# Opening batches of a fused LRU, attention and MoE kernel: u turned two batches ahead, v a batch later in y's banks, half of the normalised rows by ScalarE

## The chip, the cores and the metric

One Trainium2 chip, one core. The metric is the device time of the launch in microseconds; lower is better. The kernel before takes 1007.23 us (median of three runs, 1007.21 to 1008.69).

## The reference

x has 4 batches of 1024 tokens with 128 channels, all in float32. Two residual blocks follow each other:

```python
x = x + lru(layernorm(x))          # Bu = u B^T, scan with Lambda over the 1024 tokens, y = Re(C x) + D u
x = x + ffn(layernorm(x))
# ffn(a):
h = a + attention(rmsnorm(a, ln1_w))        # 16 heads of 8 channels, softmax over 1024 tokens
h = h + moe(rmsnorm(h, ln2_w))              # 8 experts, 256 hidden, top 2
```

The change lies in the first block and in what prepares attention: layernorm of x (called u), Bu, the scan, y, the residual sum, the second layernorm and rmsnorm in one (called a), and the projections q, k and v of a.

## The kernel before

**Stages.** The program has an opening (0 to about 160 us of the profile), in which the four batches go through the LRU and the projections, then sixteen groups of four heads ("quads") of attention, then the experts. Only the opening is touched. A batch is 8 tiles of 128 tokens. Every engine has its instruction order written out by hand, and the engines meet through semaphores that count up; a wait is for a count.

**A batch in the opening.** For batch b:

- u_nat, the normalised x, is made by VectorE for batch 0 and by ScalarE (`norm_u`, L870) for batches 1 to 3.
- TensorE turns its eight tiles into PSUM banks 0 and 1 (`first_half`, L1491), ScalarE copies them to `u_T` (`save_u`, L855), and four matmuls make Bu in banks 2 to 5 (L1498).
- VectorE (`states`, L1146) multiplies Bu by cosine and sine (L1149, L1150, from PSUM), adds the two (L1152, both operands in SBUF), scans (L1153) and multiplies the states by cosine and sine in two halves (L1156, L1157). Each half releases half of the y product (`z_ready`).
- TensorE makes y in banks 6 and 7 (`product_y`, L1511). `u_T` of the same batch is one of its operands.
- VectorE (`norm_a`, L1159) adds y to xacc (L1164), takes means and variances, forms the roots with thirteen tiny chained instructions, and writes a_nat, eight tiles (L1185). It has L1164 to L1185 and then, at once, L1149 of the next batch in its queue.
- GpSimd (`keep_z`, L574) waits for the eight tiles of a_nat and then makes zres from xacc in two instructions over the whole batch (L567, L569). After that come the lower bfloat16 parts of q and k (`lower_parts`, L584, L586), which wait for VectorE's `split_part` (L1194).
- TensorE turns a_nat into banks 0 and 1 (`turn_a`, L1536), ScalarE copies that to a_T with a scale (L899), TensorE makes q and k in banks 2 to 5 (L1541), and ScalarE rounds them to bfloat16 (L904). SyncE sends the parts to DRAM. v (`project_v`, L1547) goes to banks 0 and 1, from which ScalarE copies it into vall (L911).

**The order of TensorE.** `second_half(b)` holds, for b from 0 to 2: turn u of b + 1, Bu of b + 1, turn a of b, q and k of b, y of b + 1, v of b, and last the wait for ScalarE's copy of v:

```python
def second_half(b):
    first_half(b + 1)
    turn_a(b)
    ...
    product_y(b + 1)
    project_v(0, TILES).then_inc(v_done, 1)
    pe.wait_ge(v_saved, b + 1)
```

Since v, the turned u and the turned a share banks 0 and 1, the next batch's u can't be turned before v has been copied out. `last_half(3)` mixes the last batch's turn and projections with the first score rows of attention (L1522), the maxima of which VectorE takes (L1203), and with matmuls whose result nobody reads (L1567).

Of the kernel before, what the change touches and what calls it, by code (L numbers as in the profile page):

```python
# [10 lines left out]
ALU = mybir.AluOpType  # L11
# [58 lines left out]
def build_program(nc, x, nu2, theta2, gamma_row, b_pack, b_swap, c_re_t, c_im_t, d_t, ln1, ln2,  # L70
# [3 lines left out]
    with ctx:  # L74
# [49 lines left out]

        u_nat, u_T, a_nat, a_T = (ws[:, i, :] for i in range(4))

# [71 lines left out]
        def rows_for(t):  # L198
# [15 lines left out]
            sem(n) for n in ("u_turned", "bu_done", "y_done", "a_turned", "qk_done", "v_done"))  # L214
        uT_saved, aT_saved = sem("uT_saved"), sem("aT_saved")
        u_ready, z_ready, z_kept, a_ready = sem("u_ready"), sem("z_ready"), sem("z_kept"), sem("a_ready")
        hi_ready = sem("hi_ready")
# [607 lines left out]
        def _(act):  # L825
# [27 lines left out]
            def save_u(b):  # L853
                act.wait_ge(u_turned, b + 1)
                act.activation(u_T, bank(0, 2), ACT.Copy).then_inc(uT_saved, 1)  # L855

# [37 lines left out]

            def act_batch(b, has_next, first=False):
                if has_next:
                    save_u(b + 1)
                act.wait_ge(a_turned, b + 1)
                act.activation(a_T, bank(0, 2), ACT.Copy, scale=ln1c[:, 0:1]).then_inc(aT_saved, 1)  # L899
                if not first:  # L900
                    act.wait_ge(parts_out, b * (16 * 2 * PARTS * NQ))
                for w in range(2):
                    act.wait_ge(qk_done, b * 2 + (w + 1))
                    act.activation(parts[:, w, 0, :], bank(2 + 2 * w if has_next else 2, 2), ACT.Copy,  # L904
                                   scale=(scale, 1.0)[w]).then_inc(hi_ready, 1)
                if b + 2 < B:
                    norm_u(b + 2)
                act.wait_ge(v_done, b + 1)
                for half in range(2):
                    for j in range(NQ):  # L910
                        ins = act.activation(  # L911
                            vall[:, bass.ds(b * NQ + j, 1), half * 4:half * 4 + 4, :].rearrange("p a t c -> p (a t) c"),
                            ps[:, half, :].rearrange("p (t c) -> p t c", t=4)[:, :, 32 * j:32 * j + 32], ACT.Copy)
                ins.then_inc(v_saved, 1)

            save_u(0)
            norm_u(1)
            later_squares()
            act_batch(0, True, first=True)
            for b in range(1, B - 1):  # L920
                act_batch(b, True)
            act_batch(B - 1, False)


# [132 lines left out]
        def _(dve):  # L1057
# [101 lines left out]
            def norm_a(step, b):  # L1159
# [318 lines left out]
        def _(pe):  # L1478
# [7 lines left out]

            def first_half(b, first=False):
# [4 lines left out]
                ins.then_inc(u_turned, 1)  # L1492
                pe.wait_ge(uT_saved, b + 1)
                if not first:
                    pe.wait_ge(rest_left, b * 2)
                for i in range(2):
                    for half in range(2):
                        ins = pe.matmul(bank(2 + 2 * i + half), wB[:, i, :], u_T[:, half * 512:(half + 1) * 512],  # L1498
                                        start=True, stop=True)
                ins.then_inc(bu_done, 1)  # L1500

            def product_y(b):

                for t in range(TILES):
# [3 lines left out]
                    o = bank(6, 2)[:, c]  # L1508
                    for k, (lhs, rhs) in enumerate(((x_cos, wC[:, 0, :]), (x_sin, wC[:, 1, :]), (u_T, wD[:, :]))):
# [32 lines left out]

            def project_v(t0, t1):

                for t in range(t0, t1):
                    c = slice(t * P, (t + 1) * P)
                    ins = pe.matmul(bank(0, 2)[:, c], a_T[:, c], wv[:, :], start=(t % 4 == 0), stop=True,  # L1547
                                    skip_group_check=True)
                return ins

            def second_half(b):

                first_half(b + 1)
                turn_a(b)
                pe.wait_ge(aT_saved, b + 1)
                pe.wait_ge(bu_read, b + 2)
                for i, w in enumerate((wq, wk)):
                    project_half(w, 2 + 2 * i, 0)
                    project_half(w, 2 + 2 * i, 1).then_inc(qk_done, 1)
                product_y(b + 1)  # L1560
                project_v(0, TILES).then_inc(v_done, 1)
                pe.wait_ge(v_saved, b + 1)

# [41 lines left out]

            first_half(0, first=True)
            product_y(0)
            for b in range(B - 1):
                second_half(b)
            last_half(B - 1)  # L1610
# [279 lines left out]
```

## Time and profile before

| | |
|---|---|
| median of 3 runs | 1007.23 us |
| the profiled execution | 1007.67 us |
| its span, first to last instruction | 1005.9 us |
| around the span | 1.8 us |
| TensorE busy | 867.5 us, 86% |
| VectorE busy | 854.6 us, 85% |
| ScalarE busy | 690.2 us, 69% |
| GpSimd busy | 400.4 us, 40% |
| granted TensorE clock, mean | 0.968 of 2.4 GHz |

PE is TensorE's matmul side, PEld its weight loads, DVE VectorE, ACT ScalarE, POOL GpSimd, SP SyncE. L1152 is line 1152 of the kernel. A float32 matmul is counted as two instructions (x8 for four matmuls). The first number of a timeline row is the start in us from the span's start, the second its length, and brackets give the idle time before it with what ended it.

### The profile page before, as it was taken

The numbers are of one execution on the slowest core, as the hardware profiler recorded it, in microseconds if no ns is written. First come the engines' busy times: TensorE is split into PE (matmuls) and PEld (weight loads), VectorE is DVE, ScalarE is ACT, GpSimd is POOL, SyncE is SP. The second block draws the span as 40 slices with busy tenths as digits, with TensorE's granted clock in tenths as the row PEclk, the third lists the DMA queues.
The fourth block names the chain that finished last, engine by engine and source line by source line (L and its number), as shares of the span: only waits on it lengthen the run. The fifth ranks groups of instructions, "written<-read, shape, count | busy, mean of one in ns | idle before, by whom it ended". The sixth has DMA issues, their size and how long they took to land.

```text
span 1005.9 us, 18290 instructions
## 1 busy us (share of the span) xinstructions
PE 867.5 (86%) x5968; PEld 361.7 (36%) x5968; DVE 854.6 (85%) x1463; ACT 690.2 (69%) x1471; POOL 400.4 (40%) x621
## 2 busy tenths in 40 slices
PE   0377788999999999999999999999999999989990
PEld 0155541222222223222222322222322246588990
DVE  4978889999999998988999898898799976768663
ACT  2614313888888888888888888888788875555660
POOL 7224441011010153533615443363577503346774
PEclk9789996999999999999999999999999999999995
DMA  9997643011010110100101010110101021122346
GB/s 313 387 362 192 165 111 90 9 26 28 13 25 10 32 25 9 46 9 26 38 25 25 9 46 10 33 46 10 24 31 39 18 48 48 44 63 69 105 145 198
DMA packets 60829, 74.34 MB, mean 74 GB/s; under 512 B 9152, under 2 KB 39104, under 8 KB 60352
## 3 DMA queue, kind: packets, MB, share of 16 engines
q1 hardware_dynamic: 53936, 62.93, 21.4%
q0 software_dynamic: 4608, 9.58, 2.8%
q8 instruction: 49, 0.80, 0.3%
q10 hardware_dynamic: 2192, 0.66, 0.3%
q14 instruction: 44, 0.36, 0.1%
HBM read 28.09 MB, written 44.79 MB: 72 GB/s over the span
## 4 chain that ended last, share of the span: by engine, by line
PE 60%; DVE 25%; ACT 7%; issue 5%; ACTq 1%; POOL 1%; DMA 1%; POOLq 0%; DVEq 0%; SPq 0%
PE ps L1634 21%; DVE nmax L1203 13%; PE ps L1624 10%; PE ps L1522 9%; PE ps L1736 7%; ACT prob L961 6%; PE ps L1752 3%; PE ps L1511 3%; PE ps L1697 2%; POOL by_token L810 1%; DVE wk L1153 1%; ACTq L836 1%; PE ps L1657 1%; PE ps L1716 1%; PE ps L1498 1%
## 5 line engine op out<-in xcount | busy, mean ns | idle before, releaser
L1203 DVE TENSOR_REDUCE nmax<-ps 128x1 f32<-128x1024 f32 x512 | 601.8, 1219 | 43.9 <-PE ps L1522 39.5
L961 ACT ACTIVATE prob<-ps 128x512 f32<-128x512 f32 x1024 | 529.6, 604 | 90.6 <-PE ps L1624 89.0
L1522 PE MATMUL ps<-packs 50*128 50x512 bf16 x1024 | 343.0, 389 | 9.7 <-DVE nmax L1203 5.4
L1624 PE MATMUL ps<-packs 50*128 50x512 bf16 x1024 | 312.1, 384 | 30.2 <-ACT prob L961 20.8
L1634 PE MATMUL ps<-prob,vpad 128*32 128x512 f32 x2048 | 273.6, 606 | 0.0
L1522 PEld LDWEIGHTS ps<-packs 50*128 50x128 bf16 x1024 | 74.8, 94 | 240.4 <-DVE nmax L1203 184.9
L1624 PEld LDWEIGHTS ps<-packs 50*128 50x128 bf16 x1024 | 75.9, 94 | 144.8 <-ACT prob L961 94.1
L544 POOL MEMSET packs<- 2x2048 bf16 x32 | 57.5, 1796 | 171.1 <-PE ps L1624 169.9
L810 POOL DMA_INDIRECT by_token<-wk,vall x80 | 80.1, 1001 | 96.1 <-DVE wk L1293 61.4
L1736 PE MATMUL ps<-ws 128*128 128x128 f32 x640 | 87.2, 280 | 2.9 <-DVE ws L1313 2.1
L1736 PEld LDWEIGHTS ps<-ws 128*128 128x128 f32 x640 | 78.6, 193 | 8.7 <-issue 7.0
L1634 PEld LDWEIGHTS ps<-prob,vpad 128*32 128x32 f32 x2048 | 40.3, 108 | 60.2 <-issue 58.1
L1752 PE MATMUL ps<-w,ws 128*128 x320 | 50.6, 282 | 3.3 <-DVE wk L1293 3.1
L646 POOL TENSOR_TENSOR zres<-zres,front 128x512 f32<-128x512 f32 x6 | 7.6, 1269 | 108.4 <-ACT front L936 108.2
L1752 PEld LDWEIGHTS ps<-w,ws 128*128 128x128 f32 x320 | 42.4, 193 | 11.3 <-issue 11.2
L1004 ACT ACTIVATE ws<-ps 128x256 f32<-128x256 f32 x58 | 22.2, 383 | 32.8 <-PE ps L1736 31.8
L1286 DVE TENSOR_TENSOR ws<-ps,ws 128x256 f32<-128x256 f32 x58 | 24.5, 422 | 21.7 <-ACT ws L1004 19.2
L1511 PE MATMUL ps<-wC,wk 128*128 128x128 f32 x128 | 22.2, 301 | 21.9 <-DVE wk L1157 21.9
L1313 DVE COPY ws<-w 128x512 f32 x80 | 34.2, 430 | 7.3 <-issue 4.6
L731 POOL DMA_INDIRECT by_expert_rows<-front,slots x32 | 31.2, 976 | 11.0 <-issue 7.6
L680 POOL TENSOR_TENSOR front<-logit 128x64 f32<-128x64 f32 x24 | 6.2, 292 | 66.5 <-ACT logit L940 66.5
L1491 PE MATMUL ps<-ident,ws 128*128 128x128 f32 x32 | 5.2, 314 | 28.6 <-DVE wB L1110 25.5
(300 smaller groups left out, 857.8 us busy)
## 6 DMA issues: line engine op xcount, KB each, us to landing
by_expert_rows<-prob SPq DMA_DIRECT2D x4, 5016.0 KB, 36.8
packs<-k_parts SPq DMA_DIRECT2D x32, 192.0 KB, 3.6
packs<-q_parts SPq DMA_DIRECT2D x64, 96.0 KB, 3.1
vall<-by_expert_rows SPq DMA_DIRECT2D x80, 66.0 KB
packs<-by_token SPq DMA_DIRECT2D x8, 512.0 KB, 5.4
w<-w_t SPq DMA_DIRECT2D x3, 1024.0 KB, 10.7
q_parts<-front SPq DMA_DIRECT2D x16, 192.0 KB, 3.1
k_parts<-front SPq DMA_DIRECT2D x16, 192.0 KB, 3.4
```

The lines of the kernel that those rows point to most:

```text
L544: gp.memset(qpack[r:r + MAX_PARTS, slot, :, :, :], 0.0).then_inc(q_clear, 1)
L731: gp.indirect_dma_start(by_expert_rows, bass.IndirectOffsetOnAxis(ap=slots[:, t % 2, n % 2, n // 2:n // 2 + 1], axis=0), rows_for(t)[:, n ...
L810: gp.indirect_dma_start(by_token, bass.IndirectOffsetOnAxis(ap=dest[:, group, k:k + 1], axis=0), y_nat[:, group % YR, k * H:(k + 1) * H], ...
L961: act.activation(prob[:, v % RING, :], bank(col_bank(pos)), ACT.Exp).then_inc(col_free, 1)
L1203: dve.tensor_reduce(nmax[:, half, par, pair, qt:qt + 1], bank(first, 2), AX_X, ALU.max, negate=True).then_inc(row_free, 1)
L1313: dve.tensor_copy(w_tile[:, j % 3, :].rearrange("p (n c) -> p n c", n=2), w13[:, :, bass.ds(here[j], 1), :].rearrange("p n a c -> p n (a c ...
L1511: ins = pe.matmul(o, lhs[:, c], rhs, start=(k == 0 and t % 4 == 0), stop=(k == 2), skip_group_check=True)
L1522: ins = pe.matmul(bank(first + kh), qpack[r:r + ROWS, slot, half, pair, qt * P:(qt + 1) * P], kpack[r:r + ROWS, slot, pair, kh * HALF:(kh ...
L1624: pe.matmul(bank(col_bank(pos)), kpack[r:r + ROWS, slot, head // 2, kt * P:(kt + 1) * P], qpack[r:r + ROWS, slot, half, head // 2, :], sta ...
L1634: pe.matmul(ps[32 * head:32 * head + VW, PV_BANK, :], vpad[:, q % 2, kt, head, :], prob[:, v % RING, :], start=(kt == 0), stop=(kt == TILE ...
L1736: ins = pe.matmul(ps[:, up_bank(j), n * P:(n + 1) * P], w_tile[:, j % 3, n * P:(n + 1) * P], x_T[:, group % 2, k * P:(k + 1) * P], start=( ...
L1752: ins = pe.matmul(ps[:, y_bank(j), 0:H], hid[:, j % 4, c * P:(c + 1) * P], w2[:, bass.ds(e, 1), c, :].rearrange("p a h -> p (a h)"), start ...
```

## The change

- `u_T` becomes two buffers, taken by b % 2. TensorE turns u of batch b + 2 where it turned u of b + 1 (`turn_u`), and Bu of b + 1 (`product_bu`) finds its u_T saved long before. u of batch 1 is turned before the y of batch 0.
- v of batch b - 1 is projected in batch b, after Bu of b + 1, into y's banks 6 and 7, once VectorE has added y to xacc; the next y waits for ScalarE's copy of it. v of batch 2 stays in banks 0 and 1 after y of 3, and batch 3 is as before.
- Of the eight tiles of a_nat, VectorE makes four (tiles 0 to 3) and ScalarE the other four, each as one ACTIVATE Identity with a scale and a bias from two per-partition columns. The bias, minus mean times root, is one new VectorE instruction (`off_a`, 128x4), which also releases ScalarE (`roots_ready`).
- ScalarE's `norm_u` runs a batch earlier.

```diff
-        u_nat, u_T, a_nat, a_T = (ws[:, i, :] for i in range(4))
+        u_nat, u_even, a_nat, a_T = (ws[:, i, :] for i in range(4))
+        u_T = (u_even, sb("u_odd", [P, L])[:, :])
+        off_a = sb("off_a", [P, 2, 4])
...
-                act.activation(u_T, bank(0, 2), ACT.Copy).then_inc(uT_saved, 1)
+                act.activation(u_T[b % 2], bank(0, 2), ACT.Copy).then_inc(uT_saved, 1)
...
+            def norm_a(b):
+                act.wait_ge(roots_ready, b + 1)
+                for t in range(4, TILES):
+                    act.activation(a_nat[:, t * H:(t + 1) * H], xacc[:, b * TILES + t, :], ACT.Identity,
+                                   bias=off_a[:, b % 2, t - 4:t - 3],
+                                   scale=roots[:, b % 2, 3 * TILES + t:3 * TILES + t + 1]).then_inc(a_ready, 1)
...
+            def act_batch(b):
+                last = b == B - 1
+                if b + 2 < B:
+                    save_u(b + 2)
+                norm_a(b)
+                act.wait_ge(a_turned, b + 1)
+                act.activation(a_T, bank(0, 2), ACT.Copy, scale=ln1c[:, 0:1]).then_inc(aT_saved, 1)
+                if 1 <= b < B - 1:
+                    save_v(b - 1, 6)
+                if b:
+                    act.wait_ge(parts_out, b * (16 * 2 * PARTS * NQ))
+                for w in range(2):
+                    act.wait_ge(qk_done, b * 2 + (w + 1))
+                    act.activation(parts[:, w, 0, :], bank(2 if last else 2 + 2 * w, 2), ACT.Copy,
+                                   scale=(scale, 1.0)[w]).then_inc(hi_ready, 1)
+                if b + 3 < B:
+                    norm_u(b + 3)
+                if b >= B - 2:
+                    save_v(b, 0)
...
-                for t in range(TILES):
+                dve.scalar_tensor_tensor(off_a[:, b % 2, :], stats[:, 4:TILES, 0], -1.0, y[:, TILES + 4:2 * TILES],
+                                         ALU.mult, ALU.mult).then_inc(roots_ready, 1)
+                for t in range(4):
                     dve.tensor_scalar(a_nat[:, t * H:(t + 1) * H], tile(xacc, b, t), stats[:, t, 0:1],
                                       y[:, TILES + t:TILES + t + 1], ALU.subtract, ALU.mult).then_inc(a_ready, 1)
...
-            def second_half(b):
-
-                first_half(b + 1)
+            def batch(b):
+
+                if b + 2 < B:
+                    turn_u(b + 2)
+                product_bu(b + 1)
+                if b:
+                    pe.wait_ge(y_taken, b + 1)
+                    project_v(0, TILES, first=6).then_inc(v_done, 1)
+                if b + 2 < B:
+                    pe.wait_ge(uT_saved, b + 3)
                 turn_a(b)
                 pe.wait_ge(aT_saved, b + 1)
                 pe.wait_ge(bu_read, b + 2)
                 for i, w in enumerate((wq, wk)):
                     project_half(w, 2 + 2 * i, 0)
                     project_half(w, 2 + 2 * i, 1).then_inc(qk_done, 1)
+                pe.wait_ge(v_saved, b)
+                pe.wait_ge(y_taken, b + 1)
                 product_y(b + 1)
-                project_v(0, TILES).then_inc(v_done, 1)
-                pe.wait_ge(v_saved, b + 1)
+                if b == B - 2:
+                    project_v(0, TILES).then_inc(v_done, 1)
+                    pe.wait_ge(v_saved, b + 1)
```

TensorE between y of batch 1 and y of batch 2 (u_nat, u_T, a_nat and a_T are slices of ws), before:

```order
L1547 MATMUL ps<-wv,ws 128x128 x8
L1491 MATMUL ps<-ident,ws 128x128 [waits u_ready,v_saved]
L1491 MATMUL ps<-ident,ws 128x128 x7
L1498 MATMUL ps<-ws,wB 128x512 [waits rest_left,uT_saved]
L1498 MATMUL ps<-ws,wB 128x512 x3
L1536 MATMUL ps<-ident,ws 128x128 [waits a_ready]
L1536 MATMUL ps<-ident,ws 128x128 x7
```

and now (L1513 turns u, L1522 is Bu, L1571 v, L1560 turns a):

```order
L1513 MATMUL ps<-ident,ws 128x128 [waits u_ready]
L1513 MATMUL ps<-ident,ws 128x128 x7
L1522 MATMUL ps<-ws,wB 128x512 [waits rest_left,uT_saved]
L1522 MATMUL ps<-ws,wB 128x512 x3
L1571 MATMUL ps<-wv,ws 128x128 [waits y_taken]
L1571 MATMUL ps<-wv,ws 128x128 x7
L1560 MATMUL ps<-ident,ws 128x128 [waits a_ready,uT_saved]
L1560 MATMUL ps<-ident,ws 128x128 x7
```

v has moved from ahead of Bu to behind it, and the wait for v's copy no longer stands ahead of the turn of u.

VectorE from the last root to Bu of the next batch, before:

```order
L60 SCALAR_TENSOR_TENSOR roots<-roots 128x16 [waits dve_self]
L1185 TENSOR_SCALAR ws<-xacc,mv,roots 128x128 [waits dve_self]
L1185 TENSOR_SCALAR ws<-xacc,mv,roots 128x128 x7
L1149 TENSOR_TENSOR wk<-ps,att 128x1024 [waits bu_done]
L1150 TENSOR_TENSOR wk<-ps,att 128x1024
L1152 TENSOR_TENSOR wk<-wk 128x1024 [waits dve_self]
```

and now:

```order
L60 SCALAR_TENSOR_TENSOR roots<-roots 128x16 [waits dve_self]
L1204 SCALAR_TENSOR_TENSOR off_a<-mv,roots 128x4 [waits dve_self]
L1207 TENSOR_SCALAR ws<-xacc,mv,roots 128x128 x4
L1169 TENSOR_TENSOR wk<-ps,att 128x1024 [waits bu_done]
L1170 TENSOR_TENSOR wk<-ps,att 128x1024
L1172 TENSOR_TENSOR wk<-wk 128x1024 [waits dve_self]
```

Four of eight instructions went to ScalarE and one small one came; what used to be L1149, L1150 and L1152 is L1169, L1170 and L1172 in the changed program.

ScalarE in batch 1, before:

```order
L855 ACTIVATE ws<-ps 128x1024 [waits u_turned]
L899 ACTIVATE ws<-ps,ln1c 128x1024 [waits a_turned]
L904 ACTIVATE front<-ps 128x1024 [waits qk_done,parts_out]
L904 ACTIVATE front<-ps 128x1024 [waits qk_done]
L862 ACTIVATE ws<-xacc,rx 128x128 x8
L867 ACTIVATE ws<-ws,rx 128x128 [waits centred]
L867 ACTIVATE ws<-ws,rx 128x128 x7
L911 ACTIVATE vall<-ps 128x128 [waits v_done]
L911 ACTIVATE vall<-ps 128x128 x7
```

and now:

```order
L858 ACTIVATE u_odd<-ps 128x1024 [waits u_turned]
L902 ACTIVATE ws<-xacc,off_a,roots 128x128 [waits roots_ready]
L902 ACTIVATE ws<-xacc,off_a,roots 128x128 x3
L922 ACTIVATE ws<-ps,ln1c 128x1024 [waits a_turned]
L911 ACTIVATE vall<-ps 128x128 [waits v_done]
L911 ACTIVATE vall<-ps 128x128 x7
L929 ACTIVATE front<-ps 128x1024 [waits qk_done,parts_out]
L929 ACTIVATE front<-ps 128x1024 [waits qk_done]
```

The copy of v stands between a_T and q now, and four tiles of a_nat ahead of a_T.

## Rows read from the trace of the kernel before

**Rows 1.** Chain of waits, first two y products and batch 1's turn (start, us, what)

```profile
51.90 8.57 PE ps L1511 x48
...
76.76 5.62 PE ps L1511 x48
82.38 1.80 PE ps L1547 x16
84.20 1.47 ACT vall L911 x8
85.72 1.11 PE ps L1491 x8
...
87.93 3.71 PE ps L1498 x8
```

**Rows 2.** Timeline of VectorE, batch 0 and then batch 1

```profile
65.66 0.17 DVE L60 SCALAR_TENSOR_TENSOR roots<-roots 128x16 f32<-128x16 f32 x1
65.87 2.14 DVE L1185 TENSOR_SCALAR ws<-xacc,mv,roots 128x128 f32<-128x128 f32 x8
...
70.42 2.63 DVE L1152 TENSOR_TENSOR wk<-wk 128x1024 f32<-128x1024 f32 x1
73.08 2.29 DVE L1153 TENSOR_TENSOR_SCAN wk<-lam,wk 128x1024 f32<-128x1024 f32 x1
...
88.10 2.14 DVE L1185 TENSOR_SCALAR ws<-xacc,mv,roots 128x128 f32<-128x128 f32 x8
91.67 1.23 DVE L1149 TENSOR_TENSOR wk<-ps,att 128x1024 f32<-128x1024 f32 x1 [1.43 <-PE ps L1498]
...
94.17 1.22 DVE L1152 TENSOR_TENSOR wk<-wk 128x1024 f32<-128x1024 f32 x1
95.43 2.29 DVE L1153 TENSOR_TENSOR_SCAN wk<-lam,wk 128x1024 f32<-128x1024 f32 x1
```

**Rows 3.** Timeline of GpSimd, zres of batch 0 and batch 1

```profile
68.09 1.90 POOL L567 TENSOR_TENSOR zres<-xacc,mv 128x1024 f32<-128x1024 f32 x1 [14.33 <-DVE ws L1185]
70.07 1.90 POOL L569 TENSOR_TENSOR zres<-zres,roots 128x1024 f32<-128x1024 f32 x1
...
92.30 1.90 POOL L569 TENSOR_TENSOR zres<-zres,roots 128x1024 f32<-128x1024 f32 x1
```

**Rows 4.** Groups of ScalarE by shape, 25 to 161 us (busy us, mean ns)

```profile
L862 ACT ACTIVATE ws<-xacc,rx 128x128 f32<-128x128 f32 x24 | 7.3, 389 | 0.0
...
L885 ACT ACTIVATE vall<-xacc 128x128 f32<-128x128 f32 x16 | 4.7, 292 | 0.0
```

**Rows 5.** Timelines of VectorE and GpSimd, both in SBUF near 48 us

```profile
48.23 2.29 DVE L1153 TENSOR_TENSOR_SCAN wk<-lam,wk 128x1024 f32<-128x1024 f32 x1
...
47.69 0.57 POOL L604 TENSOR_TENSOR rx<-rx 128x16 f32<-128x16 f32 x1
48.35 2.19 POOL L605 TENSOR_TENSOR rx<-rx 128x16 f32<-128x16 f32 x1
```

**Rows 6.** Timelines of VectorE and TensorE, the end of the opening

```profile
132.80 2.14 DVE L1185 TENSOR_SCALAR ws<-xacc,mv,roots 128x128 f32<-128x128 f32 x8
134.86 4.61 DVE L1203 TENSOR_REDUCE nmax<-ps 128x1 f32<-128x1024 f32 x4
...
135.00 1.09 PE L1536 MATMUL ps<-ident,ws 128*128 128x128 f32 x8 [1.24 <-DVE ws L1185]
...
137.26 0.60 PE L1522 MATMUL ps<-packs 50*128 50x512 bf16 x2 [0.53 <-DVE nmax L1203]
...
138.24 1.02 PE L1541 MATMUL ps<-ws,wq 128*128 128x512 f32 x2
```

**Rows 7.** Timeline of ScalarE, the first exponentials of attention

```profile
167.84 4.26 ACT L961 ACTIVATE prob<-ps 128x512 f32<-128x512 f32 x8 [7.93 <-PE ps L1624]
```

**Rows 8.** Busy time of the engines in a stretch; timeline of TensorE in it

```profile
70.00:76.70 6.70, 3.67 (x8) 1.44 (x8) 6.49 (x6) 3.85 (x9) 1.90 (x1) 1.00 0.86 267
...
76.76 0.71 PE L1511 MATMUL ps<-wC,wk 128*128 128x128 f32 x4 [2.61 <-DVE wk L1157]
```

More of the change, by code:

```diff
@@ L215, in build_program @@
         uT_saved, aT_saved = sem("uT_saved"), sem("aT_saved")
+        roots_ready = sem("roots_ready")
         u_ready, z_ready, z_kept, a_ready = sem("u_ready"), sem("z_ready"), sem("z_kept"), sem("a_ready")
@@ L893, in later_squares, with save_v @@
                 act.wait_ge(squares, 1)
[L895 to L907, printed above, removed]
+            def norm_a(b):
[4 more added lines that the diff above has]
+                                   scale=roots[:, b % 2, 3 * TILES + t:3 * TILES + t + 1]).then_inc(a_ready, 1)
+            def save_v(b, first):
                 act.wait_ge(v_done, b + 1)
@@ L912, in act_batch @@
                             vall[:, bass.ds(b * NQ + j, 1), half * 4:half * 4 + 4, :].rearrange("p a t c -> p (a t) c"),
-                            ps[:, half, :].rearrange("p (t c) -> p t c", t=4)[:, :, 32 * j:32 * j + 32], ACT.Copy)
+                            ps[:, first + half, :].rearrange("p (t c) -> p t c", t=4)[:, :, 32 * j:32 * j + 32], ACT.Copy)
                 ins.then_inc(v_saved, 1)
+            def act_batch(b):
[17 more added lines that the diff above has]
+                    save_v(b, 0)
             save_u(0)
@@ L918, in _ @@
             later_squares()
[L919 to L922, printed above, removed]
+            save_u(1)
+            norm_u(2)
+            for b in range(B):
+                act_batch(b)
             def col_copy(name, q, k):
@@ L1484, in _, with turn_u @@
             pe.wait_ge(b_scaled, 4)
-            def first_half(b, first=False):
+            def turn_u(b):
                 pe.wait_ge(u_ready, b * TILES + TILES)
@@ L1492, in first_half, with product_bu @@
                 ins.then_inc(u_turned, 1)
+            def product_bu(b):
                 pe.wait_ge(uT_saved, b + 1)
-                if not first:
-                    pe.wait_ge(rest_left, b * 2)
+                pe.wait_ge(rest_left, b * 2)
                 for i in range(2):
                     for half in range(2):
-                        ins = pe.matmul(bank(2 + 2 * i + half), wB[:, i, :], u_T[:, half * 512:(half + 1) * 512],
+                        ins = pe.matmul(bank(2 + 2 * i + half), wB[:, i, :], u_T[b % 2][:, half * 512:(half + 1) * 512],
                                         start=True, stop=True)
@@ L1508, in product_y @@
                     o = bank(6, 2)[:, c]
-                    for k, (lhs, rhs) in enumerate(((x_cos, wC[:, 0, :]), (x_sin, wC[:, 1, :]), (u_T, wD[:, :]))):
+                    for k, (lhs, rhs) in enumerate(((x_cos, wC[:, 0, :]), (x_sin, wC[:, 1, :]), (u_T[b % 2], wD[:, :]))):
                         ins = pe.matmul(o, lhs[:, c], rhs, start=(k == 0 and t % 4 == 0), stop=(k == 2),
@@ L1541, in project_half, with project_v @@
                 return pe.matmul(bank(o + half), w[:, :], a_T[:, half * 512:(half + 1) * 512], start=True, stop=True)
-            def project_v(t0, t1):
+            def project_v(t0, t1, first=0):
                 for t in range(t0, t1):
                     c = slice(t * P, (t + 1) * P)
-                    ins = pe.matmul(bank(0, 2)[:, c], a_T[:, c], wv[:, :], start=(t % 4 == 0), stop=True,
+                    ins = pe.matmul(bank(first, 2)[:, c], a_T[:, c], wv[:, :], start=(t % 4 == 0), stop=True,
                                     skip_group_check=True)
                 return ins
-            def second_half(b):
-                first_half(b + 1)
+            def batch(b):
[7 more added lines that the diff above has]
+                    pe.wait_ge(uT_saved, b + 3)
                 turn_a(b)
@@ L1604, in last_half @@
                 score_unit(11)
-            first_half(0, first=True)
+            turn_u(0)
+            product_bu(0)
+            turn_u(1)
             product_y(0)
             for b in range(B - 1):
-                second_half(b)
+                batch(b)
             last_half(B - 1)
```

## The prediction

> **What bounds the kernel now.** I read the chain of waits first, because it names who is late at each handover, and of it only the opening, since nothing else is edited. In batch 1 it runs from y through v, the copy of v, the turn of u, the copy of u and Bu [rows 1], and only then reaches VectorE's L1149: 9.29 us from the end of y (82.38) to 91.67. Next, the timeline of VectorE [rows 2]. The engine is nearly always busy here. It waits 1.43 us for Bu in batch 1; in batch 0 it doesn't wait for it at all, and batch 2 repeats batch 1 to within 0.02 us in every step. So the chain through v that looks 9.29 us long is late by only 1.43 us: beside it VectorE works through the roots and L1185. Last, the timeline of GpSimd beside it, since L1152 of batch 0 takes 2.63 us where it takes 1.22 us in batch 1 [rows 2]. In batch 0 it starts at 70.42, while GpSimd's L569 runs from 70.07 to 71.97, and ends 1.08 us after that. In batch 1 GpSimd ends at 94.20 [rows 3] and L1152 starts at 94.17. The wait for Bu there has kept the two apart by chance.
>
> I count from T, the start of the instruction that follows the last root (L1185 before, off_a after). What matters is how long after T the scan starts: 7.21 us in batch 0 (73.08 less 65.87), 7.33 us in batch 1 (95.43 less 88.10) [rows 2] and in batch 2. From the scan to the next T the path isn't edited: scan, states, y, sums, roots.
>
> **Part 1: u two batches ahead, v later.** Bu of the next batch now needs only the turn of u (1.11 us, and none of it in batch 2) and Bu itself (3.71 us) after y [rows 1]: it is done 4.8 us after y's end. T comes 5.72 us after it (88.10 less 82.38) and L1149 later still. The wait of 1.43 us goes in batches 1 and 2 and nothing takes its place at Bu. v (1.80 us) follows Bu, so TensorE is free 6.6 us after y's end, that is T + 0.9, before a_nat is there (below). The copy of v (1.47 us) is queued behind a_T on ScalarE and ahead of the copy of q. It ends near T + 5.8, TensorE's q is done near T + 6.1, and y doesn't start before T + 10, so both waits for v cost nothing; if ScalarE were 4 us late y would pay. The copy of u sits ahead of the tiles of a_nat on ScalarE, and is done long before T, since a copy of that size takes about 1 us. SyncE's DMAs aren't moved.
>
> **Part 2: half of a_nat by ScalarE.** VectorE loses four of eight instructions, each 0.27 us (2.14 over 8 [rows 2]), and gains one of 128x4. A tiny one such as L60 of the roots takes 0.17 us [rows 2], of which some 0.1 stays before the next unchained one can start. L1149 thus starts at T + 0.1 + 1.07 = T + 1.17 and L1152, 2.50 us behind it (94.17 less 91.67 [rows 2]), wants to start at T + 3.67.
>
> ScalarE's price isn't in this trace: no ACTIVATE here has both a pointer scale and a pointer bias. With neither, 128x128 takes 0.292 us, with one 0.389 [rows 4]. Bounds: a second pointer costs nothing, and four take 1.26 us (a start every 0.292, as eight of L862 in 2.43 us); or it costs another 0.097 in each, unhidden, and four take about 3 x 0.39 + 0.48 = 1.64 us. I take 1.64, since the first pointer costs that much. a_nat is whole at T + 0.17 + 0.07 (a handover) + 1.64 = T + 1.88, against T + 2.14 before.
>
> The Trainium skill has a price for this (ScalarE: Activation LUTs, What ACT_TABLE_LOAD costs): about 93 ns for each pointer operand, and neighbours overlap by 93 ns. By it the four take the same 1.64 us; no row here has two pointers.
>
> **Part 3: what the gain runs into.** Without anything else the scan would start at T + 3.67 + 1.26 = T + 4.93 and the three batches would gain 2.28 + 2 x 2.40 = 7.1 us. But GpSimd's zres starts when a_nat is whole, at T + 1.96, and takes 1.90 + 0.08 + 1.90 us [rows 3]. L567 lasts to T + 3.86, and L1152 comes at T + 3.67. That is the meeting of batch 0, now in every batch. From the rows: an instruction with two operands in SBUF waits for GpSimd's to end (2.63 us, batch 0), and the reverse holds too: GpSimd's L605, 128x16, takes 2.19 us beside the scan and ends at 50.54, as the scan does at 50.52; L604 ends at 48.26, just after L1152 and as the scan starts [rows 5]. So whoever waited gets the turn at the next boundary. Then L1152 runs from T + 3.86 to T + 4.94, L569 waits for that and runs its 1.8 us to T + 6.76, and the scan, issued at T + 4.97, ends as if it had started at T + 6.61 (L1152 too ends 0.15 us sooner after a release than its full length). Against 7.21 once and 7.33 twice that is 0.60 + 2 x 0.72 = **2.0 us** of gain where 7.1 stood.
>
> What speaks for reading it so is also a rule of the Trainium skill (SBUF — State Buffer, Who interferes with whom): a VectorE instruction with two SBUF inputs and a GpSimd instruction that reads SBUF take one shared port as an exclusive lock, and the second to issue fully blocks. The trace agrees, with 2.63 us against 1.22. By this rule the sum is the one below; with no such lock it would be 7.1 + 0.8.
>
> **Part 4: the last batch.** a_nat of batch 3 is followed by VectorE's maxima. They start at T + 1.17 instead of T + 2.06 (134.86 less 132.80). The turn of a starts at T + 1.95 instead of T + 2.20, its copy ends near T + 4.2, and the fourth score row (137.26, T + 4.46), which waits for the second maximum, moves to T + 3.55. The q projection, before at T + 5.44 [rows 6], then waits for a_T and four unread matmuls (0.44 us): T + 4.66. That is **0.8 us**. Bounds: 0.9 where VectorE alone decides, 0.25 where the turn does. Behind it the opening is one chain of projections, maxima and SyncE's queue which moves as a whole, and the first exponential waits for TensorE [rows 7], not for the zero fill.
>
> **Sum.** 2.0 + 0.8 = 2.8 us. The profiled execution of 1007.67 us would be 1004.9; it stands 0.44 us above the median, so the median goes from 1007.23 to 1004.4. With ScalarE at its lower bound GpSimd starts 0.38 us sooner, and the gain becomes up to 3.6. About 0.2%, 2 us, is what a measurement of this kernel tells from no change.
>
> **The rivals.**
> - *The lock falls out badly.* L1152 waits for both L567 and L569, as happens if L569 is let in first: it ends at T + 5.84 + 1.08, the scan starts at T + 6.95, and the three batches give 0.26 + 2 x 0.38 = 1.0. For it: batch 0 of before shows just such a full wait. Against: L569 is issued 0.08 us after L567, when L1152 already waits. 1007.2 - 1.8 = 1005.4.
> - *VectorE keeps the port.* The scan is issued 0.03 us after L1152 and goes ahead of L569, which waits for both. The scan starts at T + 4.97, the gain is 2.24 + 2 x 2.36 + 0.8 = 7.8, the time 999.5. For it: all four scans take 2.29 us, none was ever held up. Against: L604, which slipped in between.
> - *The later part takes it back.* If attention started by something that isn't moved, the time would stay at 1007.2. Against: the wait of rows 7 is for TensorE.
> - *Slower: TensorE's clock.* With q and k done at T + 7.9 and y not before T + 10.2, TensorE idles 2.3 us ahead of every y, where batch 1 had 1.2. The first y, after a long idle stretch, took 8.57 us at the lower clock of 1.2 GHz, the next 5.62 us [rows 1]. If the clock fell in each of three batches it would cost 3 x 2.95 = 8.9, less 2.8: 1013.3. It decides from one batch on (2.95 against 2.8). Against: in batch 0 TensorE idled 2.61 us ahead of y with the granted clock at 1.00, that is 2.4 GHz [rows 8].
>
> **How the numbers follow.** Forecast 0.50, bad lock 0.20, port kept 0.14, taken back 0.09, clock 0.07. Time 1004.4. Faster by over 0.2% (below 1005.2) are four fifths of the forecast, the kept port and a fifth of the bad lock: 0.40 + 0.14 + 0.04, rounded up to 0.60. Slower is the clock and a little for things not seen: 0.08. The rest is 0.32. The range leaves out the kept port at its full size and the clock: 1001.0 to 1007.0, room at the lower end for a port kept in one or two batches.
>
> **What would show it.** L1149's counterpart without a wait for Bu in every batch; four ACTIVATEs of about 0.48 us; the add (L1152) longer than 1.22 us and the scan longer than 2.29 us or GpSimd's second zres instruction longer than 1.90 us in batches 0 to 2; the step from T to T, 22.23 us from batch 0 to 1 now, 0.6 to 0.7 us shorter. I am wrong if that step is 20 us (port kept), if y takes over 6 us at a clock below 1.00, or if the projections of v hold y back.

## The result and the profile after

The changed kernel takes 1005.19 us (median of ten runs, 1003.35 to 1007.06), the kernel before beside it on the same chip 1008.84 us (ten runs, 1007.19 to 1010.37). The ratio is 0.996, with a 95% interval of 0.9952 to 0.9968: 4.0 us faster, 3.2 to 4.8. That is faster by over 0.2%, as forecast. The 2.8 us of the sum lies a little below the interval. Two of the runs reported below, 1048.42 us of the kernel before on the third chip and 1330.82 us of the last variant, were in a slow state at a mean granted clock of 0.836 and 0.562, and the ratios leave them out.

| | before | after |
|---|---|---|
| profiled execution, us | 1007.67 | 1006.17 |
| span, us | 1005.9 | 1004.4 |
| T of batches 0 to 3, us | 65.87, 88.10, 110.47, 132.80 | 64.75, 87.21, 108.76, 130.31 |
| steps from T to T, us | 22.23, 22.37, 22.33 | 22.46, 21.55, 21.55 |
| first exponential, us | 167.84 | 164.54 |
| mean granted clock | 0.968 | 0.963 |

The engines' busy time, the first part of the page, hardly moves: TensorE has 4.7 us more (867.5 before), with a mean clock a little lower, and GpSimd 2.6 us more (400.4 before), which is three times the 0.86 us that its second zres instruction takes longer (below).

```profile
PE 872.2 (87%) x5968; PEld 364.4 (36%) x5968; DVE 854.3 (85%) x1451; ACT 696.9 (69%) x1487; POOL 403.0 (40%) x621
```

T is the start of the instruction after the last root, as in the prediction. The timeline of VectorE in batch 1 of the changed kernel answers to [rows 2]:

```profile
87.21 0.16 DVE L1204 SCALAR_TENSOR_TENSOR off_a<-mv,roots 128x4 f32<-128x4 f32 x1
87.29 1.11 DVE L1207 TENSOR_SCALAR ws<-xacc,mv,roots 128x128 f32<-128x128 f32 x4
88.32 1.22 DVE L1169 TENSOR_TENSOR wk<-ps,att 128x1024 f32<-128x1024 f32 x1
89.45 1.21 DVE L1170 TENSOR_TENSOR wk<-ps,att 128x1024 f32<-128x1024 f32 x1
90.81 1.31 DVE L1172 TENSOR_TENSOR wk<-wk 128x1024 f32<-128x1024 f32 x1
92.15 3.87 DVE L1173 TENSOR_TENSOR_SCAN wk<-lam,wk 128x1024 f32<-128x1024 f32 x1
96.05 0.69 DVE L1176 TENSOR_TENSOR wk<-wk,att 128x512 f32<-128x512 f32 x1
```

L1169 follows with no wait for Bu. The scan is issued at T + 4.94, and takes 3.87 us where all four took 2.29. GpSimd beside it answers to [rows 3]:

```profile
89.14 1.90 POOL L570 TENSOR_TENSOR zres<-xacc,mv 128x1024 f32<-128x1024 f32 x1 [5.40 <-ACT ws L902]
91.12 2.76 POOL L572 TENSOR_TENSOR zres<-zres,roots 128x1024 f32<-128x1024 f32 x1
```

Read the four as a queue for one door, the access to SBUF that the prediction calls the port. L570 ends at 91.04 and L1172, issued at 90.81, ends 1.08 us later. L572 is issued at 91.12 and ends at 93.88, 1.76 after L1172's end (92.12). The scan is issued at 92.15 and ends at 96.02, 2.14 after L572's end. Each waits out the other's instruction, whole. L1169 and L1170, which read PSUM, keep their 1.22 us beside L570, and L570 its 1.90.

The price of ScalarE's four tiles, in its groups by line, where [rows 4] had no such form:

```profile
L902 ACT ACTIVATE ws<-xacc,off_a,roots 128x128 f32<-128x128 f32 x16 | 6.6, 482 | 21.7 <-DVE off_a L1204 21.7
```

Batch 0 isn't shorter in this trace. The timeline of TensorE there:

```profile
66.74 1.94 PE L1560 MATMUL ps<-ident,ws 128*128 128x128 f32 x8 [3.10 <-ACT ws L902]
69.88 3.78 PE L1565 MATMUL ps<-ws,wq 128*128 128x512 f32 x4 [1.20 <-ACT ws L922]
73.46 3.12 PE L1565 MATMUL ps<-ws,wk 128*128 128x512 f32 x4
76.41 0.61 PE L1535 MATMUL ps<-wC,wk 128*128 128x128 f32 x4
```

and the busy time of the engines in two stretches of it (after the length: PE, PEld, DVE, ACT and POOL busy with counts, the granted clock, DMA share, GB/s):

```profile
66.70:76.00 9.30, 8.06 (x16) 4.11 (x17) 9.09 (x8) 2.14 (x2) 4.63 (x2) 0.50 0.79 282
76.00:82.00 6.00, 5.93 (x50) 5.50 (x48) 4.04 (x9) 5.35 (x16) 4.55 (x4) 1.00 0.98 238
```

After 3.10 us without work the granted clock is 0.50, that is 1.2 GHz, for the turn, q and most of k. q and k together take 6.70 us (69.88 to 76.58) instead of the 3.67 of [rows 8], and y begins at 76.41 (T + 11.66) though the states of its first half are ready at 74.9; in batch 1 it begins at T + 10.28. Of these 1.4 us VectorE hides 0.5, since it has the rounding of q and k to do meanwhile. The first T, on the other hand, is 1.12 us earlier than before. Two unplanned things, then, beside the planned ones; the experiments have to say which belong to the change.

The end of the opening, which answers to [rows 6] and [rows 7] (timelines of VectorE, TensorE and ScalarE):

```profile
130.31 0.16 DVE L1204 SCALAR_TENSOR_TENSOR off_a<-mv,roots 128x4 f32<-128x4 f32 x1
...
134.95 1.02 PE L1565 MATMUL ps<-ws,wq 128*128 128x512 f32 x2
...
164.54 4.26 ACT L981 ACTIVATE prob<-ps 128x512 f32<-128x512 f32 x8 [7.93 <-PE ps L1660]
```

The q projection runs at T + 4.64, and what follows moves as a whole. Attention carries the 3.3 us of its start through: the last copy of its output starts at 879.9 before and at 876.7 after. Behind it 1.7 us of the 3.2 are lost again in these two executions: from that copy to the end are 126.0 us before and 127.7 after, so that the spans differ by 1.5 us only. The 4.0 us of the runs isn't the difference of these two traces.

### The profile page after: what moved, and what is told of

It reads as the page before. It is cut to its first block, busy times and chain, and to the rows that moved or that the text cites. A ratio compares the mean times of both kernels' runs of the same rounds, so it can differ in the third digit from the quotient of the medians.

```text
span 1004.4 us, 18298 instructions
## 1 busy us (share of the span) xinstructions
PE 872.2 (87%) x5968; PEld 364.4 (36%) x5968; DVE 854.3 (85%) x1451; ACT 696.9 (69%) x1487; POOL 403.0 (40%) x621
## 4 chain that ended last, share of the span: by engine, by line
PE 58%; DVE 26%; ACT 8%; issue 5%; ACTq 1%; POOL 1%; DMA 1%; POOLq 0%; DVEq 0%; SPq 0%
PE ps L1670 21%; DVE nmax L1225 13%; PE ps L1660 9%; PE ps L1546 8%; ACT prob L981 7%; PE ps L1772 7%; PE ps L1788 3%; PE ps L1535 2%; PE ps L1733 2%; PE ps L1565 1%; DVE wk L1173 1%; POOL by_token L813 1%; ACTq L839 1%; PE ps L1693 1%; PE ps L1752 1%
## 5 line engine op out<-in xcount | busy, mean ns | idle before, releaser
L1024 ACT ACTIVATE ws<-ps 128x256 f32<-128x256 f32 x58 | 22.3, 384 | 34.3 <-PE ps L1772 33.0
L1513 PE MATMUL ps<-ident,ws 128*128 128x128 f32 x32 | 5.1, 312 | 26.3 <-DVE wB L1130 25.7
```

## The experiments

Line numbers are those of each kernel. "Before" is always measured beside the variant on the same chip. The first four are of one chip, on which the kernel before took 1009.08 us (median of 29 runs); the two other chips are marked. The second (from the two fillers to the changed kernel again) took 1065.83 us for the kernel before (median of 27). Its openings agree with the others' to about 0.2 us; of the 53 us by which the changed kernel is longer in its trace there, about 20 come between the first exponential and the last copy of attention's output and 33 behind it, where nothing is edited. Compare ratios there, and times of the opening. Each variant has one trace, so a statement on its steps is one on that execution.

**The new order alone.** The changed kernel, with all eight tiles on VectorE:

```diff
-                norm_a(b)
...
-                dve.scalar_tensor_tensor(off_a[:, b % 2, :], ...).then_inc(roots_ready, 1)
-                for t in range(4):
+                for t in range(TILES):
```

> The changed kernel with all eight tiles of a_nat made by VectorE again; u two batches ahead and v a batch later stay. Port theory (an instruction with two SBUF operands and GpSimd's zres exclude each other): L1149's counterpart no longer waits for Bu, but the add behind it then meets zres in batches 1 and 2 as it does in batch 0 of before, takes about 2.6 us, and the scan starts at T + 7.2 instead of T + 7.3: the step from T to T stays within 0.2 us of 22.37 us, and the whole kernel is within 1 us of before. Rival (the gain of the change is the wait for Bu that went): the step falls by 1.4 us in two batches, and the kernel is 2.8 us faster than before. The turn of u of batch 1 ahead of the first y should still let that y end about 1 us sooner than in before; TensorE idles over 3 us ahead of the turn of a in batch 0, so q and k there should run at the lower clock.

Measured 1008.39 us, ratio 0.999 (0.9982 to 0.9999). The timeline of VectorE, batch 1:

```profile
87.25 2.14 DVE L1204 TENSOR_SCALAR ws<-xacc,mv,roots 128x128 f32<-128x128 f32 x8
89.31 1.22 DVE L1168 TENSOR_TENSOR wk<-ps,att 128x1024 f32<-128x1024 f32 x1
...
91.80 2.62 DVE L1171 TENSOR_TENSOR wk<-wk 128x1024 f32<-128x1024 f32 x1
94.46 2.29 DVE L1172 TENSOR_TENSOR_SCAN wk<-lam,wk 128x1024 f32<-128x1024 f32 x1
```

The wait of 1.43 us is gone and the add takes 2.62 in place of 1.22, 1.40 of it given straight to the shared access. The steps are 22.25, 22.22 and 22.24 us, all of them batch 0's old step. v's move and the second u_T bring 0.1 us in batches 1 and 2 by themselves (22.22 and 22.24 for 22.37 and 22.33), and from the first T to the first exponential 0.23 us (101.74 for 101.97).

**The split alone.** The kernel before, with off_a, ScalarE's four tiles and `range(4)`:

```diff
                 save_u(b + 1)
+                norm_a(b)
...
-                for t in range(TILES):
+                dve.scalar_tensor_tensor(off_a[:, b % 2, :], ...).then_inc(roots_ready, 1)
+                for t in range(4):
```

> The kernel before with only the split of a_nat (four tiles by ScalarE, off_a). Port theory and part sum: batch 0 gains 0.6 us, batches 1 and 2 nothing, because VectorE then waits some 2.4 us for Bu (which still follows v, its copy and the turn of u), and by then zres is over; the last batch gains 0.8 us. In all 1.4 us faster than before. Rival (what counts is VectorE's busy time, four instructions of 0.27 us a batch less): 1 us in each of four batches, 4 us faster, all of what the change gives.

Measured 1009.45 us, ratio 0.9997 (0.9988 to 1.0006): nothing, where 1.4 us were expected. Batch 0 is as expected (21.55, scan 3.87), although its q is slow too (3.53 us). The next two steps are 24.04 and 24.06 instead of 22.3. Timelines of TensorE and VectorE, and the stretch of Bu:

```profile
85.99 5.40 PE L1511 MATMUL ps<-ws,wB 128*128 128x512 f32 x8 [1.11 <-ACT ws L857]
...
91.43 1.23 DVE L1160 TENSOR_TENSOR wk<-ps,att 128x1024 f32<-128x1024 f32 x1 [4.07 <-PE ps L1511]
...
86.00:89.00 3.00, 3.00 (x4) 1.36 (x5) 1.32 (x6) 1.65 (x4) 0.91 (x1) 0.53 0.36 88
```

Bu runs at the low clock for much of its length and takes 5.40 us instead of 3.71 [rows 1]. All of that lies on the path. The last batch gives its 0.8 us here too (from the last T to the first exponential 34.23 us for 35.04). From the first T to the first exponential it is 103.88 us, 1.9 more than before; without the 1.7 us in each of two batches it would be the 1.4 less that were expected. What makes the clock drop there the trace doesn't say; see late zres in the kernel before.

**zres out of the opening.** The changed kernel, in which GpSimd makes zres of batch q later, behind the zero fill of quad q, when VectorE no longer needs the access; mv and roots are kept for all batches so that they live that long:

```diff
-        mv = sb("mv", [P, 2, TILES, 2])
-        roots = sb("roots", [P, 2, 3 * 2 * TILES])
+        mv = sb("mv", [P, B, TILES, 2])
+        roots = sb("roots", [P, B, 3 * 2 * TILES])
...
-                keep_z(b, b)
...
+                keep_z(q, q)
+                gp.wait_ge(z_kept, q + 1)
...
-                if b >= 2:
-                    dve.wait_ge(z_kept, b - 1)
```

> The changed kernel with GpSimd's zres moved out of the opening, behind the refill of quads 0 to 3 (mv and roots get a buffer for each batch). Port theory: the scan takes 2.29 us again and the add 1.22 us, the step from T to T falls from 21.55 us to about 19.7 us in batches 1 and 2; in batch 0 nothing is gained while TensorE's q and k at the lower clock hold the y product. In all about 3.7 us faster than the changed kernel, 7.5 us faster than before. Rival (the long scan is slow for another reason, such as DMA traffic on SBUF): the scan stays at 3.9 us and the time doesn't move.

Measured 1003.87 us, ratio 0.9944 (0.9931 to 0.9957), by the ratios 1.6 us below the changed kernel. VectorE, batch 1:

```profile
87.19 0.16 DVE L1203 SCALAR_TENSOR_TENSOR off_a<-mv,roots 128x4 f32<-128x4 f32 x1
...
90.79 1.22 DVE L1173 TENSOR_TENSOR wk<-wk 128x1024 f32<-128x1024 f32 x1
92.05 2.29 DVE L1174 TENSOR_TENSOR_SCAN wk<-lam,wk 128x1024 f32<-128x1024 f32 x1
...
107.07 0.16 DVE L1203 SCALAR_TENSOR_TENSOR off_a<-mv,roots 128x4 f32<-128x4 f32 x1
```

Add and scan have their full speed in every batch. Steps 21.30, 19.88 and 21.23: the middle one is what the port leaves behind, 1.67 us less than with zres. The two others carry a slow q and k (3.78 and 2.36 us in batch 0, 3.78 and 2.21 in batch 2), for which y waits. In batch 2 of the changed kernel q is slow as well (3.29 us), but there y starts 0.69 us after k has ended. A shorter batch leaves less room, so I had the clock wrong in batch 2, and of the 3.7 us that I expected on top of the changed kernel's gain only 1.6 came.

**Work that nobody reads, ahead of the turn.** The changed kernel with matmuls whose result nobody reads, 24, none and 16 of them:

```diff
+            FILLER = (24, 0, 16)
...
                     pe.wait_ge(uT_saved, b + 3)
+                unused_products(FILLER[b])
                 turn_a(b)
```

> The changed kernel with matmuls that nobody reads in TensorE's idle stretch ahead of the turn of a: 24 in batch 0, 16 in batch 2. Clock theory: TensorE stays at 2.4 GHz in batch 0, q and k take 3.7 us instead of 6.7 us there, and y starts as soon as its states are ready, 1.7 us sooner than in the changed kernel; batch 2 gains nothing, since its q and k just end before y is ready. In all 1.7 us faster than the changed kernel. Rival (the clock falls for another reason, or y isn't held by k): no difference, or slower by up to 0.5 us where the fillers run over the moment at which a is ready.

Measured 1006.75 us, ratio 0.9973 (0.9962 to 0.9983). The timeline of TensorE, batch 0 and then the last y:

```profile
67.68 1.09 PE L1560 MATMUL ps<-ident,ws 128*128 128x128 f32 x8 [0.38 <-ACT ws L902]
69.97 1.98 PE L1565 MATMUL ps<-ws,wq 128*128 128x512 f32 x4 [1.21 <-ACT ws L922]
...
119.14 1.01 PE L1535 MATMUL ps<-wC,wk 128*128 128x128 f32 x4 [2.38 <-DVE wk L1177]
```

The idle stretch ahead of the turn is 0.38 us, q takes 1.98 instead of 3.78, and batch 0's step is 21.53. The low clock went with the idle time, so it did come from that. But q and k of batch 2, now short, leave TensorE idle for 2.38 us ahead of the last y, which starts at 1.2 GHz: that step is 22.78 where it was 21.55. The clock is low for its first three tiles of eight (the granted clock is 0.55 from 119.0 to 122.5). In batch 1, ahead of which no filler stands, q is slow now (3.37 us; 1.98 in the changed kernel), at no cost. One gap closed, the next opened; the 1.7 us expected didn't come, and by the ratios the kernel is 1.3 us slower than the changed one.

**Fillers at both places** (second chip). FIRST = (24, 4, 16) ahead of the turn, and SECOND = (16, 16, 16) ahead of y:

```diff
-            FILLER = (24, 0, 16)
+            FIRST, SECOND = (24, 4, 16), (16, 16, 16)
...
+                unused_products(SECOND[b])
                 pe.wait_ge(v_saved, b)
```

> The changed kernel with unread matmuls in both idle stretches of TensorE: 24, 4 and 16 ahead of the turn of a in batches 0, 1 and 2, and 16 ahead of each y. Clock theory: in the run with one set of fillers the granted clock fell instead in the 2.4 us ahead of the last y, which cost 1.2 us; with both stretches filled it stays at 2.4 GHz from the second batch's turn on, each y starts with its states and takes 5.6 us, and all three steps from T to T are 21.5 to 21.6 us. Against the profile of the changed kernel that is 0.9 us. Rival (fillers only move the low clock about, or delay real work): one step or more stays above 22.3 us.

Steps 21.55, 21.55 and 21.54, scans 3.87; 1060.98 us, ratio 0.995 (0.9931 to 0.9969). Every q takes 1.98 us and every y starts with its states: the clock is out of the picture in this trace, and what is left is the port. In time nothing shows beside the changed kernel on the same chip (1060.41 us, ratio 0.9956). The expected 0.9 us is there in the opening: from the first T to the first exponential 98.96 us for 99.79.

**Late zres and both fillers** (second chip). The edits of the two together, with FIRST = (24, 6, 16) and SECOND = (4, 4, 4):

> Both cures together: GpSimd's zres moved behind the refills of quads 0 to 3, and unread matmuls ahead of the turn of a (24, 6, 16) and of y (4, 4, 4). Port and clock theories add: all three steps about 19.8 us, the last T about 5 us earlier than in the changed kernel, the first exponential near 159.5 us, and the kernel 4.5 to 6 us faster than the changed one. Rival (the y product waits for something else once the scan is early): steps stay at 21 us in batches 0 and 2.

Steps 19.90, 19.87 and 19.88, scans 2.29, first exponential at 159.78; 1053.99 us, ratio 0.9888 (0.9861 to 0.9916). Batch 0 of TensorE:

```profile
70.00 1.98 PE L1564 MATMUL ps<-ws,wq 128*128 128x512 f32 x4 [1.21 <-ACT ws L923]
71.82 1.88 PE L1564 MATMUL ps<-ws,wk 128*128 128x512 f32 x4
```

From the first T to the first exponential this is 93.98 us, before 101.97 [rows 2, 7]: 8.0 us. The prediction's sum without a lock was 7.1 + 0.8 = 7.9. Against the fillers with zres in place (98.96) it is 5.0 us: that is the price of the port over three batches, with the clock out of both.

**Late zres in the kernel before** (second chip). The same edit, on the kernel before alone:

> The kernel before with zres moved behind the refills. Port theory: only batch 0's add met zres there, so its step falls by 1.4 us to 20.8 us (L1149 of batch 1 still waits for Bu, which comes no sooner, so the scan keeps its place in batches 1 and 2): 1.4 us faster than before at most, and steps 2 and 3 stay at 22.3 us. Rival (the port costs before as much as after): 4 us faster.

Steps 20.84, 24.04 and 24.04; 1064.69 us, ratio 0.9988 (0.9968 to 1.0007). The first step is as expected; the others aren't 22.3. The timeline of TensorE, turn of u and Bu of batch 2 in the kernel before and then here:

```profile
85.72 1.09 PE L1491 MATMUL ps<-ident,ws 128*128 128x128 f32 x8 [1.56 <-ACT vall L911]
87.93 3.70 PE L1498 MATMUL ps<-ws,wB 128*128 128x512 f32 x8 [1.11 <-ACT ws L855]
...
82.82 1.09 PE L1490 MATMUL ps<-ident,ws 128*128 128x128 f32 x8 [1.55 <-ACT vall L912]
85.03 5.40 PE L1497 MATMUL ps<-ws,wB 128*128 128x512 f32 x8 [1.11 <-ACT ws L856]
```

It is the slow Bu of the split alone, by a different road, and without its 1.7 us in two batches the expected 1.4 us would be there. But the gaps ahead of it are those of the kernel before to 0.01 us, where Bu took 3.70 us at a granted clock of 1.00. Batch 0 has the same: gaps of 1.86 us ahead of the turn and 1.32 us ahead of q in both, and q takes 1.95 us before and 3.42 us here. So their length isn't what decides, and that a shorter batch 0 brings the slow Bu isn't shown. A rival stands: it may be a matter of the execution. The kernel before has one trace, and that with a mean clock of 0.968; of its 29 runs on the first chip 7 had 0.968 (1008.4 us on average) and 21 had 0.965 (1009.3), and on the third 15 of 17 had 0.965. If the slow Bu is in most runs of the kernel before, part of the 4.0 us is that; no trace shows it.

**The changed kernel again** (second chip), unedited:

> The changed kernel once more, to see which numbers of its trace repeat. Both theories: the adds of 1.3 us, the scans of 3.87 us and GpSimd's 2.76 us repeat to within 0.05 us, since they follow from the order alone. Clock theory: the first T (64.75 us, between 64.6 and 65.9 in the runs so far, whatever the kernel) and the batch in which TensorE runs at its lower clock may differ from run to run. If instead the clock falls at the same place to within 0.2 us, it follows from the order alone too.

Steps 22.48, 21.55 and 21.54; 1060.41 us, ratio 0.9956 (0.9937 to 0.9976). q and k of batch 0:

```profile
69.67 3.78 PE L1565 MATMUL ps<-ws,wq 128*128 128x512 f32 x4 [1.20 <-ACT ws L922]
73.25 3.14 PE L1565 MATMUL ps<-ws,wk 128*128 128x512 f32 x4
```

The same two rows to 0.02 us, on another chip.

**Late zres and both fillers again** (third chip; kernel before 1009.78 us, median of 17):

> Late zres and both sets of fillers once more, on whatever chip, beside the changed kernel. If the opening is what it gains, the steps are 19.9 us again, the last T is 4.7 us (130.1 less 125.45) ahead of the changed kernel's, and the time is 4 to 6.5 us below the changed kernel's on the same chip and 8 to 10 us below before's.

Measured 1000.90 us, ratio 0.9913 (0.9899 to 0.9927). Steps 19.88, 20.67 and 19.88. In batch 1 this time:

```profile
88.39 3.31 PE L1564 MATMUL ps<-ws,wq 128*128 128x512 f32 x4 [1.20 <-ACT ws L923]
91.49 2.30 PE L1564 MATMUL ps<-ws,wk 128*128 128x512 f32 x4
```

The same six unread matmuls stand ahead of that turn as in the trace before, where q took 1.98 us; here they weren't enough, and y was held up by 0.8 us. From the first T to the last it is 60.43 us, 4.2 less than the 64.64 of the changed kernel's trace on this chip, where 4.7 were expected; to the first exponential it is 94.75 us.

**The changed kernel a third time** (third chip):

> The changed kernel on the same chip as the combined one. By the order the steps are 22.5, 21.55 and 21.55 us, with q and k of batch 0 at the lower clock. Clock by chance (rival): the slow batch is another one this time.

Measured 1005.88 us, ratio 0.9966 (0.9953 to 0.9979). Steps 21.56, 21.54 and 21.54, from a first T of 65.91:

```profile
70.59 3.78 PE L1565 MATMUL ps<-ws,wq 128*128 128x512 f32 x4 [1.20 <-ACT ws L922]
74.17 2.41 PE L1565 MATMUL ps<-ws,wk 128*128 128x512 f32 x4
...
91.73 3.27 PE L1565 MATMUL ps<-ws,wq 128*128 128x512 f32 x4 [1.20 <-ACT ws L922]
```

q is slow here too, but the clock rises within k and the step is what the port allows. q of batch 1 is slow as well, which it isn't in the two other traces, at no cost. So the low clock in batch 0 is there in all three traces, and its cost in two of them.

**Late zres and both fillers, without the split** (third chip): the combination with the first experiment's edit, all eight tiles on VectorE:

> The combined kernel with all eight tiles of a_nat made by VectorE again. With port and clock out of the way the split should be worth its VectorE time: four instructions of 0.256 us less the 0.1 us of off_a, 0.9 us in each of three steps (20.8 us) and 0.8 us in the last batch, 3.6 us in all. Rival (the split pays only in company, as its run alone suggested): steps stay within 0.2 us of 19.9 us. If the port's lock comes back in any form, the adds are longer than 1.22 us.

Steps 20.98, 20.84 and 20.84, scans 2.29; 1005.22 us, ratio 0.9956 (0.9941 to 0.9971). From the first T to the first exponential it is 97.68 us against 93.98 with the split: 3.70 us for the split, the lock being out of the way. Against the second trace with the split, 94.75 with its slow q and k, it is 2.9 us. By the ratios the split is worth 4.3 us here. Within the lock its worth in a batch is the order's step less the whole's, 22.22 to 21.55: 0.67 us.

## Why the prediction was right, step by step

Time, range and sign held: 1004.4 forecast, 1005.19 measured. That the time is so near is partly luck, for two deviations cancel: the kernel before took 1.6 us more than the median that the forecast started from, and the gain is 1.2 us more than the sum. The sum itself is met by the traces of the opening, which give 2.2, 2.2 and 3.1 us from the first T to the first exponential where it says 2.8. What the runs say of each step:

- **Part 1, the wait for Bu goes in batches 1 and 2 and nothing replaces it at Bu.** Right, in all traces of the new order. What replaced it stood one instruction further: with the order alone the add gave 1.40 of the 1.43 us back. v's copy never held y.
- **Part 2, ScalarE's price.** Right: 0.482 us for an ACTIVATE with two pointers (0.48 taken), 1.65 us for four (1.64 taken). VectorE's first product starts at T + 1.11 (T + 1.17), GpSimd at T + 1.92 to 1.93 (T + 1.96).
- **Part 3, alternation at the port.** Right in its mechanism, and of nearly the right size. The add ran from T + 3.60 to T + 4.91 (3.86 to 4.94 forecast as its own turn), and the states were through the scan at T + 8.81 to T + 8.82 against T + 9.50 and 9.62: 0.69 + 0.81 + 0.81 = 2.3 us where 2.0 stood. In batch 0 this gain reached the next T only in the third trace of the changed kernel; in the two others the slow q and k took it (below). The rule of the Trainium skill on which the reading leaned (SBUF — State Buffer, Who interferes with whom) holds in every trace that has zres in the opening: whoever comes second blocks whole. With zres moved away, add and scan had 1.22 and 2.29 us throughout. For the 7.9 us of the sum without a lock the opening gave 8.0 in one trace and 7.2 in the other, which has a slow q and k.
- **Part 4, the last batch.** Right: q projection at T + 4.64 (4.66 forecast, 5.44 before), 0.80 us, and the rest moved as one chain. The split alone shows the same 0.8 us. The rival that attention would take it back is out.
- **The rival that VectorE keeps the port** didn't occur: no step of 20 us with zres in place. **The bad lock** neither: L572 never went in ahead of the add.
- **The rival of TensorE's clock** occurred in part, at another place and at a third of its price. The prediction had the idle time ahead of y in mind, and put y at the low clock at 2.95 us, the first y's 8.57 less 5.62. That price is too small for a whole y: the first y of the kernel before has the granted clock 0.50 only to 58.0 us, its tiles starting 1.28 us apart, and then 0.67 us apart. By these an estimate for eight slow tiles is 4.9 us. What ran slow was q and k, after the 3.10 us in which TensorE waits for a_nat. Part 1 had TensorE free at T + 0.9, which holds where v stands between Bu and the turn; v of batch -1 doesn't exist, so in batch 0 it was free at T - 1.1. It cost 0.9 us in one batch of the profiled execution (a step of 22.46 where 21.55 is what the port allows) and nothing in the third trace. A y that began at the low clock, the thing feared, came only with a filler.

The sum against the trace: the first exponential is 3.30 us earlier. First T +1.12, batch 0 -0.23, batches 1 and 2 +0.82 and +0.78, the rest +0.81. The +1.12 isn't the change's: the first T lies between 64.3 and 65.9 us in the eleven experiments' traces and the two first ones, whichever kernel, by how early the clock rises within the first y (at about 58.0 us in the kernel before, between 55 and 56 us in the changed kernel's first trace), and the changed kernel gave 64.75, 64.54 and 65.91, the kernel before 65.87 and, with one edit each, 64.62 and 64.37. But an early first T and the hold-up in batch 0 nearly cancel: T of batch 1 is 87.21, 87.02 and 87.47 in those three. In the third trace, whose first T is that of the kernel before, the change is worth 3.1 us to the first exponential (167.84 less 164.78).

The parts don't add up. From the first T to the first exponential the order alone gains 0.2 us, the split alone loses 1.9, and the whole gains 2.2 to 3.1; by the ratios it is 1.0 us, 0.3 us (no change, by its interval) and 4.0 us. The order alone frees VectorE and hands the gain to the port, as its expectation said. The split alone gains in batch 0 and in the last batch, waits for Bu in between, as expected, and there met the slow Bu, which was foreseen nowhere.

What stays open: the 4.0 us of the runs is 0.9 us more than the best of the three traces of the opening gives, and no trace places the difference. The spans of two traces of the same kernel differ by up to 2 us behind the first exponential (839.9 us in the changed kernel's first trace, 838.0 in its third; 838.1 in that of the kernel before), without a cause that these runs show. So differences under 1 us between kernels are taken from the opening's own rows here and not from the medians. Why the clock falls in one handover of 1.1 us and not in the next was not settled either.

The best version is late zres with both fillers: 1000.90 us beside 1005.88 for the changed kernel on the same chip, and 1053.99 beside 1060.41 on the other, 5.0 and 6.4 us less.

## What to carry to other kernels

Before you count a wait as gained, look at which engine's instructions stood apart only because of it: here GpSimd's two passes over a batch met VectorE's add and scan as soon as the wait for Bu had gone, and about five of eight microseconds went there. Work of GpSimd that nobody needs soon belongs where VectorE rests or reads PSUM (L570 beside L1169 cost neither of them anything). And when a chain of handovers is shortened, read TensorE's granted clock in the stretches between them again: a product can run slow and, in a shorter batch, hold up the next. Traces of one execution each don't settle the clock: take several of the same kernel, the one before included.

## What the hardware did that I had not expected

- TensorE's clock fell with little idle time. In the split alone and in late zres on the old order, Bu took 5.40 us instead of 3.71 with 1.11 us without work just ahead of it. Ahead of that are the eight matmuls of the turn, and ahead of those another gap of 1.55 us; the granted clock was 0.53 in the first 3 us of Bu in the split alone. The kernel before has the same two gaps (1.56 and 1.11 us) and the clock at 1.00. So the gaps just ahead of a product don't tell at which clock it runs. The Trainium skill (TensorE: Matmul & The Clock Gate, Why this matters for your kernels) warns of idle gaps between bursts of matmuls. The 3.10 us ahead of the changed kernel's turn agree with it; this Bu ran slow after much shorter ones, and the measurement decides.
- Which matmuls run slow is nearly the same from trace to trace, yet not quite. In all three traces of the changed kernel q is slow in batch 0 (3.78 us) and in batch 2 (3.28 to 3.44), in batch 1 only in the third (3.27 for 1.98). In the combination it is q and k of batch 1 in one of two traces. Without the split q of batch 0 took 3.58 us in spite of the fillers.
- VectorE's scan and its add show the lock alike: 3.87 us for 2.29 and 2.62 for 1.22. GpSimd pays as well, 2.76 us for 1.90.
